# Graph kernel, gather passes: eight 32-column products of a tile become two of 128 columns

## The chip, the cores and the metric

The kernel runs on one core of a Trainium2 chip. The metric is the device time of one execution in microseconds; before the change the median of three runs is 7301.54 (7296.5 to 7303.85). The engines are TensorE (PE; its weight loads are listed as PEld), VectorE (DVE), ScalarE (ACT), GpSimd (POOL) and SyncE (SP).

## The reference, cut to what matters

3125 nodes with 256 features, 50000 edges (sorted by target), four graph layers one after the other, each with a residual and a layer normalisation. The first and the third sum over the edges of each target node, with a softmax weight:

```
# first layer (one head)
scores = h_src @ a_s + h_tgt @ a_t
ex = exp(scores - segment_max(scores, tgt)[tgt])
agg = segment_sum(h_src * (ex / (se[tgt] + 1e-10))[:, None], tgt)
# third layer (8 heads of 32 features, self loops added)
e = leaky_relu(a_src[src] + a_dst[dst], 0.2)
ex = exp(e - segment_max(e, dst)[dst])
out = segment_sum(h[src] * alpha[:, :, None], dst)
```

The second layer has three rounds of edge attention with 4 heads, the fourth multiplies by a product of 50000 plane rotations. None of the two is touched.

## The kernel before

The program sorts the edges by blocks of nodes, builds the rotation matrix, and then runs the layers in order. The function `segment_sums` holds one gather pass; it is called twice, with tag e0 and H=1 for the first layer and with tag e2 and H=8 for the third. A block is NBD = 32 target nodes. The edges stand in TD = 496 tiles of P = 128 edges, all of one block; four tiles are a batch, so there are NBT = 124 batches, and PER = 4 batches are a group. All main-loop code is written out, without a loop on the chip, and each engine has its own order, over steps `st` = 0 to 132:

- POOL (L1064 to L1074) fetches, with one indirect DMA for each tile, the 128 rows of the source nodes into `hg`, a ring of RING = 11 batches; from the twelfth batch on it first waits for "agg" of the batch 11 before.
- SP loads one-hot rows into `stack` (L1085).
- TensorE in step `st` first turns the score columns of batch `st` (L1152, into `ps_t`), then makes the logits of batch c = st-6 (L1161, into `ps_d`), then the control product of batch st-1 (L1170, into `ps_s`; one product for H=1, two of 128x512 for H=8), in one step of four a group's products (L1182, after a wait for VectorE's group work "A"), and last the gather of batch e = c-2 (L1193 to L1201) into one of two tiles `ps_g`. In one step of four the rescaling products L1209 and L1213 follow (for H=1 one, L1216).
- VectorE in step `st` takes a maximum from `ps_s` (L1244), adds the four results of batch c-3 from `ps_g` into `accT`, one after the other, at a block address read from a table (L1265), for H=8 makes the leaky logits (L1270, L1275), then the operand `Em` of batch c-1 (L1289), and after the last batch of a group the group work (L1297 to L1327, and the splitting into three bf16 parts in L1977 to L1981). Once in four steps it makes the one-hots `hot` of a group (L1282) and `spread` (L1334).
- ScalarE copies `ps_t` into `stack` (L1104), after L1182 copies `ps_x` to `R` (L1111), and takes the exponentials `exd` (L1132 or L1135).

`hot[p, tile, n]` is 1 where edge p of a tile belongs to node n of its block. In the gather, before the change, `Em` is this one-hot times the edge's exponential: 32 columns for H=1, 8 x 32 for H=8. For each 32 features the stationary operand is 32 columns of the gathered rows, and the moving one the 32 columns of `Em` (for H=8 those of that head). The four products of a half of the features write to partitions 0, 32, 64 and 96 of `ps_g`. L1199 makes the denominators. A float32 product appears in the trace as two records.

Of the kernel before, what the change touches and what calls it, by code (L numbers as in the profile page):

```python
# [12 lines left out]
P = 128  # L13
N, D, E = 3125, 256, 50000
# [13 lines left out]
NBD = 32  # L28
# [3 lines left out]
RING, ROWS, LAG = 11, 8, 6  # L32
# [889 lines left out]
def segment_sums(nc, tag, K, H, W, htab, adtab, estab, blocks, quads, ohtab, oth, kl, accT, selftab):  # L922
# [14 lines left out]
    PER = GT // 4  # L937
    STEPS = NBT + LAG + 3
    with ExitStack() as ctx:
# [95 lines left out]
        hg = sm("hg", [P, RING, 4, W])  # L1035
# [20 lines left out]
        with ExitStack() as rs:  # L1056
# [3 lines left out]
            with phase(nc, tag + "m", names, rings) as (block, s):  # L1060
# [76 lines left out]
                @block.tensor  # L1137
                def _(pe):
                    pe.wait_ge(s["zero"], 1)
                    for i in range(2):  # L1140
                        pe.matmul(ps_g[i][:, 0:2].rearrange("p u v n -> p (u v n)"), K["zero"][:, 0:P], K["zero"][:, 0:192],
                                  start=True, stop=True, skip_group_check=True)
                        pe.matmul(ps_g[i][:, 2:4].rearrange("p u v n -> p (u v n)"), K["zero"][:, 0:P], K["zero"][:, 0:192],
                                  start=True, stop=True, skip_group_check=True)
                    for st in range(STEPS):
                        c, b = st - LAG, st - 1
                        if st < NBT:
                            pe.wait_ge(rings[st % RING], 64 * (st // RING + 1))
                            if st >= 1:
                                pe.wait_ge(s["row"], st)  # L1150
                            for u in range(4):
                                tr = pe.matmul(ps_t[ROW0:ROW0 + SPLITS * H, u, :], hg[:, st % RING, u, D:W].bitcast(BF16)[:, 0:SPLITS * H],  # L1152
                                               K["identb"][:, :], start=True, stop=True)
                            tr.then_inc(s["turn"], 1)
                        if 0 <= c < NBT:
                            if c % PER == 0:
                                pe.wait_ge(s["R"], c // PER + 1)
                            if c >= 1:
                                pe.wait_ge(s["exd" if S2 == 1 else "dc"], c)
                            for u in range(4):  # L1160
                                mm = pe.matmul(ps_d[:, u, :], stack[:, c % ROWS, u, :],  # L1161
                                               R[:, c // PER % 2, (c % PER) * 4 + u, :], start=True, stop=True)
                            mm.then_inc(s["D"], 1)
                        if 0 <= b < NBT:
                            pe.wait_ge(s["row"], b + 1)
                            pe.wait_ge(oh_s[b % ROWS], 64 * (b // ROWS + 1))
                            if b >= 1:
                                pe.wait_ge(s["peak"], b)
                            for k in range(HC):
                                mm = pe.matmul(ps_s[0:M, k].rearrange("p u e -> p (u e)"), ctl[:, k, 0:M],  # L1170
                                               stack[:, b % ROWS].rearrange("p u e -> p (u e)"), start=True, stop=True)
                            mm.then_inc(s["ctl"], 1)
                        if st % PER == 1 and st >= PER + 1 and st // PER - 1 < NG:
                            g = st // PER - 1
                            pe.wait_ge(s["A"], g + 1)
                            if g >= 1:
                                pe.wait_ge(s["R"], g)
                            if S2 > 1:
                                pe.wait_ge(s["adst"], g + 1)
                            for h in range(H4):  # L1180
                                for n in range(SPLITS):
                                    mm = pe.matmul(ps_x[n * NBD:(n + 1) * NBD, h].rearrange("p s c t -> p (s c t)"),  # L1182
                                                   K["identb"][0:M, h * NBD:(h + 1) * NBD],
                                                   B[0:M, g % 2, n].rearrange("p s c t -> p (s c t)"), start=True, stop=True,
                                                   skip_group_check=True)
                            mm.then_inc(s["sel"], 1)
                        if 0 <= c - 2 < NBT:
                            e = c - 2
                            pe.wait_ge(s["E"], e + 1)
                            if e >= 2:  # L1190
                                pe.wait_ge(s["take"], (e - 2) * 4 + 4)
                            for u in range(4):
                                lhs = lambda lo, n: hg[:, e % RING, u, lo:lo + n]  # L1193
                                for k in range(2):
                                    for h in range(4):
                                        pe.matmul(ps_g[e % 2][h * NBD:(h + 1) * NBD, u, k, :], lhs(k * P + h * NBD, NBD),  # L1196
                                                  Em[:, e % 2, u, k * 4 + h if H > 1 else 0, :],
                                                  start=True, stop=True, skip_group_check=True)
                                mm = pe.matmul(ps_g[e % 2][0:H, u, 2, :], exd[:, e % 3, u, :],  # L1199
                                               hot[:, e // PER % 2, (e % PER) * 4 + u, :], start=True, stop=True,  # L1200
                                               skip_group_check=True)  # L1201
                            mm.then_inc(s["agg"], 1)
                            if (e + 1) % PER == 0 and (e + 1) // PER < NG:
                                g = (e + 1) // PER
                                pe.wait_ge(s["spread"], g)
                                if g >= 2:
                                    pe.wait_ge(s["grow"], g - 1)
                                if H > 1:
                                    pe.matmul(ps_y[:, 0:2, :].rearrange("p v n -> p (v n)"), quad[:, :],  # L1209
                                              spread[:, g % 2].rearrange("p c n -> p (c n)"), start=True, stop=True,  # L1210
                                              skip_group_check=True)
                                    for k in range(HC):
                                        mm = pe.matmul(ps_y[:, 2, :], quadden[:, k, :], spread[:, g % 2, k, :],  # L1213
                                                       start=(k == 0), stop=(k == HC - 1), skip_group_check=True)
                                else:
                                    mm = pe.matmul(ps_y[:, 0, :], K["ones"][0:M, :], spread[0:M, g % 2, 0, :], start=True,  # L1216
                                                   stop=True)
                                mm.then_inc(s["scale"], 1)

                @block.vector  # L1220
                def _(dve):
# [17 lines left out]
                    for st in range(STEPS):  # L1239
# [37 lines left out]
                        if 0 <= c < NBT:  # L1277
                            if c % PER == 0:
                                g = c // PER
                                if g >= 2:  # L1280
                                    dve.wait_ge(s["agg"], (g - 2) * PER + PER)
                                dve.tensor_tensor(hot[:, g % 2], K["row"][:, 0:NBD].unsqueeze(1).broadcast_to([P, GT, NBD]),  # L1282
                                                  kl[:, g * GT:(g + 1) * GT].unsqueeze(2).broadcast_to([P, GT, NBD]),
                                                  ALU.is_equal).then_inc(s["hot"], 1)
                            dve.wait_ge(s["exd"], c + 1)
                            dve.wait_ge(s["hot"], h0 + c // PER + 1)
                            if c >= 2:
                                dve.wait_ge(s["agg"], c - 1)
                            dve.tensor_tensor(Em[:, c % 2],  # L1289
                                              hot[:, c // PER % 2, (c % PER) * 4:(c % PER) * 4 + 4].unsqueeze(2)  # L1290
                                              .broadcast_to([P, 4, H, NBD]),
                                              exd[:, c % 3].unsqueeze(3).broadcast_to([P, 4, H, NBD]),
                                              ALU.mult).then_inc(s["E"], 1)
                        if 0 <= b < NBT and b % PER == PER - 1:
# [1056 lines left out]
```

## Time and profile before

| | |
|---|---|
| median of three runs | 7301.54 us |
| span of the profiled execution | 9062.1 us |
| own time of the profiled execution | none listed beside the span |
| mean granted TensorE clock | 0.812 |
| PE matmul busy | 4683.8 us (52%), 60555 instructions |
| DVE busy | 5139.2 us (57%), 12108 instructions |
| POOL busy | 4305.5 us (48%), 3974 instructions |
| L1196 gather products, both passes | 15872 records, 569.9 us busy |
| L1069 indirect DMA, both passes | 992, 991.8 us busy |

The profiled execution was longer than the timed ones. A slice of the page's second part is 226.6 us. The main loop of the first gather pass lies from about 2833 to 3690 us, that of the third layer from about 7919 to 8815 us.

### The profile page before, as it was taken

How to read it: one execution, taken by the hardware profiler on the slowest of the kernel's cores; microseconds unless marked ns; L12 is line 12 of the kernel's file. 1: busy time of each engine (PE TensorE's matmuls, PEld its weight loads, DVE VectorE, ACT ScalarE, POOL GpSimd, SP SyncE). 2: the span in 40 equal slices, each digit the busy share in tenths (PEclk: the TensorE clock that was granted, in tenths of full speed). 3: DMA queues.
4: the chain of work that ended last, by engine and by line, in shares of the span. 5: the costliest groups of instructions: out<-in, count | busy, mean ns of one | idle time of the engine just before them, and what ended most of it. 6: DMA issues, size and time to landing. Idle time of an engine off the chain costs nothing. (4 is left out here: it accounts for less than half of the span.)

```text
span 9062.1 us, 179398 instructions
## 1 busy us (share of the span) xinstructions
PE 4683.8 (52%) x60555; PEld 3816.1 (42%) x60555; DVE 5139.2 (57%) x12108; ACT 1224.9 (14%) x2828; POOL 4305.5 (48%) x3974
## 2 busy tenths in 40 slices
PE   0000000488732555476766767766676777445552
PEld 0000000366621444356666556666566665323331
DVE  7996000377754444655665455555455555557767
ACT  0000000122201111111111011111011111122220
POOL 5887777200063555135655055554255552066640
PEclk9999999999955555689999889898889988755555
DMA  0000000000012333155552255551355540133320
GB/s 24 3 1 1 1 1 1 1 0 0 4 26 65 101 101 101 48 167 156 158 157 62 88 147 161 152 150 31 117 154 158 156 120 21 30 94 98 98 75 24
DMA packets 708570, 691.60 MB, mean 76 GB/s; under 512 B 234981, under 2 KB 589355, under 8 KB 708165
## 3 DMA queue, kind: packets, MB, share of 16 engines
q0 software_dynamic: 227328, 446.06, 18.1%
q1 hardware_dynamic: 480846, 240.51, 9.6%
q8 instruction: 218, 3.57, 0.2%
q14 instruction: 178, 1.46, 0.1%
HBM read 766.03 MB, written 77.58 MB: 93 GB/s over the span
## 5 line engine op out<-in xcount | busy, mean ns | idle before, releaser
L1669 POOL DMA_INDIRECT kvring<-kvtab,oth x1776 | 1834.4, 1033 | 1619.5 <-PE ea_psg L1731 923.2
L1069 POOL DMA_INDIRECT e_hg<-htab,oth_d x992 | 991.8, 1000 | 1130.9 <-issue 713.4
L1720 PE MATMUL ea_pss<-ea_qb,ea_kT 128*128 128x128 f32 x7104 | 1198.0, 306 | 0.0
L1720 PEld LDWEIGHTS ea_pss<-ea_qb,ea_kT 128*128 128x128 f32 x7104 | 1113.8, 224 | 32.3
L1790 DVE TENSOR_TENSOR acc<-ea_psg,acc 128x64 f32 x1776 | 399.0, 225 | 1161.3 <-remote 1049.8
L1731 PE MATMUL ea_psg<-ea_mix,kvring 128*64 128x64 f32 x14208 | 581.9, 240 | 887.6 <-DVE ea_mix L1832 877.2
L1731 PEld LDWEIGHTS ea_psg<-ea_mix,kvring 128*64 128x64 f32 x14208 | 522.1, 152 | 984.8 <-issue 691.2
L255 POOL DMA_INDIRECT sb_rec<-srawrec,splacei x392 | 430.9, 1099 | 960.5 <-PEq L56 815.9
L1196 PE MATMUL e_psg<-e_Em,e_hg 128*32 128x32 f32 x15872 | 569.9, 245 | 439.6 <-issue 399.4
L1764 ACT ACTIVATE ea_kT<-ea_pst 128x512 f32<-128x512 f32 x888 | 481.9, 595 | 2201.5 <-remote 1331.3
L1196 PEld LDWEIGHTS e_psg<-e_Em,e_hg 128*32 128x32 f32 x15872 | 439.2, 146 | 622.0 <-issue 524.2
L241 POOL DMA_INDIRECT steps<-or_rec,or_rplacei x392 | 568.3, 1450 | 136.0 <-issue 136.0
L1804 DVE TENSOR_REDUCE ea_sc<-ea_pss 128x64 f32<-128x1024 f32 x444 | 541.6, 1220 | 97.6 <-PE ea_pss L1720 61.8
L1717 PE MATMUL ea_pss<-mrow,ea_mk 128*128 128x256 bf16 x1776 | 547.6, 308 | 64.7 <-ACT ea_kT L1764 49.0
L1832 DVE TENSOR_TENSOR ea_mix<-ea_hot,ea_att 128x1024 f32<-128x1024 f32 (+1 forms) x444 | 544.1, 1225 | 0.1
L1708 PE MATMUL ea_pst<-ident,kvring 128*128 128x128 f32 x3552 | 464.8, 274 | 78.4 <-DMA kvring<-kvtab,oth 77.3
L1244 DVE TENSOR_REDUCE e_mt<-e_pss 32x4 f32<-32x512 f32 (+1 forms) x248 | 235.0, 948 | 465.7 <-PE e_pss L1170 371.6
L237 POOL DMA_INDIRECT sd_rec<-drawrec,dplacei x392 | 406.2, 1036 | 128.4 <-issue 126.4
L1708 PEld LDWEIGHTS ea_pst<-ident,kvring 128*128 128x128 f32 x3552 | 406.4, 142 | 80.5 <-issue 79.4
L1265 DVE TENSOR_TENSOR accT<-e_psg,accT 128x96 f32 x992 | 254.3, 256 | 253.5 <-issue 131.4
L594 DVE TENSOR_TENSOR or_T<-or_psw,or_T 128x512 f32<-128x512 f32 x97 | 66.8, 689 | 451.8 <-remote 424.7
L1199 PE MATMUL e_psg<-e_hot,e_exd 128*1 128x32 f32 (+1 forms) x1984 | 291.5, 239 | 34.9 <-issue 34.9
(506 smaller groups left out, 8250.9 us busy)
## 6 DMA issues: line engine op xcount, KB each, us to landing
ea_qb<-qtab SPq DMA_DIRECT2D x1776, 64.0 KB
qtab<-at_qst SPq DMA_DIRECT2D x75, 512.0 KB, 3.3
kvring<-kvtab,oth POOLq DMA_INDIRECT x1776
e_stack<-ohtab SPq DMA_DIRECT2D x744, 32.0 KB
kvtab<-at_kvst SPq DMA_DIRECT2D x75, 256.0 KB, 2.7
e_hg<-htab,oth_d POOLq DMA_INDIRECT x992
ea_mk<-mtab SPq DMA_DIRECT2D x444, 3.0 KB
htab<-Hd SPq DMA_DIRECT2D x2, 3200.0 KB, 11.6
```

What stands on the lines that cost most here:

```text
L241: pool.indirect_dma_start(out=rec, out_offset=bass.IndirectOffsetOnAxis(ap=placei[:, j:j + 1], axis=0), in_=rawrec[:, j, :], in_offset=Non ...
L255: pool.indirect_dma_start(out=rec, out_offset=bass.IndirectOffsetOnAxis(ap=placei[:, begin + j:begin + j + 1], axis=0), in_=rawrec[:, begi ...
L1069: pool.indirect_dma_start(out=hg[:, b % RING, u, :], out_offset=None, in_=htab, in_offset=bass.IndirectOffsetOnAxis(ap=oth[:, b * 4 + u:b ...
L1196: pe.matmul(ps_g[e % 2][h * NBD:(h + 1) * NBD, u, k, :], lhs(k * P + h * NBD, NBD), Em[:, e % 2, u, k * 4 + h if H > 1 else 0, :], start=T ...
L1669: pool.indirect_dma_start(out=kv[:, b % R, u, :], out_offset=None, in_=kvtab, in_offset=bass.IndirectOffsetOnAxis(ap=oth[:, b * QB + u:b * ...
L1708: tr = pe.transpose(ps_t[:, u, k, :], kv[:, r, u, k * P:(k + 1) * P], K["ident"][:, :])
L1717: pe.matmul(ps_s[r % 2][:, u, :], mk[:, r, u * P:(u + 1) * P], K["mrow"][:, :], start=True, stop=False, skip_group_check=True)
L1720: mm = pe.matmul(ps_s[r % 2][:, u, k * 2 * HN:(k + 1) * 2 * HN], kT[:, r % 2, u, k, :], qb[:, r, u, :], start=False, stop=True, skip_group ...
L1731: mm = pe.matmul(ps_g[r % 2][c * DH1:(c + 1) * DH1, u, :], kv[:, r, u, D + g * DH1:D + (g + 1) * DH1], mix[:, r % 2, u, g * G:(g + 1) * G, ...
L1764: ins = act.activation(kT[:, r % 2, 2 * k:2 * k + 2], ps_t[:, 2 * k:2 * k + 2], ACT.Copy)
L1804: dve.tensor_reduce(sc[:, :, :, :].rearrange("p u g h -> p (u g h)"), ps_s[r % 2][:, :, :].rearrange("p u (q n) -> p (u q) n", n=NBS), AX. ...
L1832: dve.tensor_tensor(mix[:, r % 2], hot[:, bass.ds(b * QB, QB), :].unsqueeze(2) .broadcast_to([P, QB, G * G, NBS]), att[:, :, :, :].rearran ...
```

## The change

In `segment_sums` the gather's products are regrouped. For H=1 the stationary operand is 128 features of the gathered rows at once and the moving one the 32 columns of `Em`. For H=8 VectorE multiplies the gathered rows themselves by the exponentials (each head's on its 32 features), so that `Em` is 256 weighted features; TensorE has 128 of these columns as stationary operand, and the one-hots of the tile, unweighted, as the moving one. The result in `ps_g` stands at the same place as before.

```diff
@@ -1190,14 +1190,16 @@
                             for u in range(4):
-                                lhs = lambda lo, n: hg[:, e % RING, u, lo:lo + n]
+                                nodes = hot[:, e // PER % 2, (e % PER) * 4 + u, :]
                                 for k in range(2):
-                                    for h in range(4):
-                                        pe.matmul(ps_g[e % 2][h * NBD:(h + 1) * NBD, u, k, :], lhs(k * P + h * NBD, NBD),
-                                                  Em[:, e % 2, u, k * 4 + h if H > 1 else 0, :],
+                                    if H > 1:
+                                        pe.matmul(ps_g[e % 2][:, u, k, :], Em[:, e % 2, u, k * 4:(k + 1) * 4, :]
+                                                  .rearrange("p h n -> p (h n)"), nodes,
                                                   start=True, stop=True, skip_group_check=True)
-                                mm = pe.matmul(ps_g[e % 2][0:H, u, 2, :], exd[:, e % 3, u, :],
-                                               hot[:, e // PER % 2, (e % PER) * 4 + u, :], start=True, stop=True,
+                                    else:
+                                        pe.matmul(ps_g[e % 2][:, u, k, :], hg[:, e % RING, u, k * P:(k + 1) * P],
+                                                  Em[:, e % 2, u, 0, :], start=True, stop=True, skip_group_check=True)
+                                mm = pe.matmul(ps_g[e % 2][0:H, u, 2, :], exd[:, e % 3, u, :], nodes, start=True, stop=True,
                                                skip_group_check=True)
@@ -1287,8 +1289,8 @@
                             dve.tensor_tensor(Em[:, c % 2],
-                                              hot[:, c // PER % 2, (c % PER) * 4:(c % PER) * 4 + 4].unsqueeze(2)
-                                              .broadcast_to([P, 4, H, NBD]),
+                                              hg[:, c % RING, :, 0:D].rearrange("p u (h d) -> p u h d", h=H) if H > 1 else
+                                              hot[:, c // PER % 2, (c % PER) * 4:(c % PER) * 4 + 4].unsqueeze(2),
                                               exd[:, c % 3].unsqueeze(3).broadcast_to([P, 4, H, NBD]),
                                               ALU.mult).then_inc(s["E"], 1)
```

## Rows read from the trace of the kernel before

**Rows 1.** The page: the span, and two rows of the 40 slices.
```profile
span 9062.1 us, 179398 instructions
...
POOL 5887777200063555135655055554255552066640
PEclk9999999999955555689999889898889988755555
```

**Rows 2.** Windows of rotations, first pass, third layer, its tail; busy, granted clock.
```profile
core 0: us, PE busy (x) PEld busy (x) DVE busy (x) ACT busy (x) POOL busy (x), PEclk, DMA share, GB/s
3200.00:3300.00 100.00, 58.88 (x1268) 41.62 (x1267) 43.32 (x152) 13.10 (x39) 58.30 (x61) 0.50 0.38 101
...
8350.00:8450.00 100.00, 57.27 (x1295) 36.75 (x1293) 73.80 (x190) 25.44 (x61) 61.48 (x59) 0.50 0.36 97
8842.00:8856.00 14.00, 8.98 (x33) 5.01 (x33) 9.41 (x13) 1.28 (x1) 0.00 (x0) 0.50 0.07 4
1900.00:2000.00 100.00, 84.70 (x1123) 68.95 (x1123) 76.47 (x185) 22.62 (x48) 0.00 (x0) 0.95 0.01 0
```

**Rows 3.** Timeline of the first pass: start, length, engine, line, operation, count, idle before.
```profile
3204.03 0.30 PE L1196 MATMUL e_psg<-e_Em,e_hg 128*32 128x32 f32 x3 [0.39 <-issue]
...
3204.52 0.95 POOL L1069 DMA_INDIRECT e_hg<-htab,oth_d  x1 [0.30 <-issue]
...
3206.25 0.24 PE L1196 MATMUL e_psg<-e_Em,e_hg 128*32 128x32 f32 x1 [0.50 <-issue]
...
3207.69 0.46 PE L1196 MATMUL e_psg<-e_Em,e_hg 128*32 128x32 f32 x16
```

**Rows 4.** Groups by form, 2900 to 3860 us: busy, mean ns, idle before, releasers.
```profile
L1069 POOL DMA_INDIRECT e_hg<-htab,oth_d x452 | 436.7, 966 | 313.0 <-PE e_psg L1199 209.7 <-issue 102.9 <-DMA e_hg<-htab,oth_d 0.3
L1196 PE MATMUL e_psg<-e_Em,e_hg 128*32 128x32 f32 x7936 | 328.9, 245 | 279.6 <-issue 268.7 <-DVE e_Em L1289 10.6
```

**Rows 5.** Timeline of TensorE in the third layer's pass.
```profile
8128.74 1.01 PE L1213 MATMUL e_psy<-e_spread,e_quadden 128*128 128x32 f32 x4
8129.68 0.60 PE L1152 MATMUL e_pst<-identb,e_hg 128*24 128x128 bf16 x4
8130.22 0.28 PE L1161 MATMUL e_psd<-e_R,e_stack 128*128 128x16 bf16 x4
8130.34 1.01 PE L1170 MATMUL e_pss<-e_stack,e_ctl 128*128 128x512 bf16 x2
8131.29 0.44 PE L1196 MATMUL e_psg<-e_Em,e_hg 128*32 128x32 f32 x16
8131.52 0.24 PE L1199 MATMUL e_psg<-e_hot,e_exd 128*8 128x32 f32 x1
...
8131.84 0.24 PE L1199 MATMUL e_psg<-e_hot,e_exd 128*8 128x32 f32 x1
...
8131.90 0.24 PE L1199 MATMUL e_psg<-e_hot,e_exd 128*8 128x32 f32 x1
```

**Rows 6.** Timeline of VectorE in the third layer's pass, over two and a half steps.
```profile
8294.13 1.22 DVE L1244 TENSOR_REDUCE e_mt<-e_pss 128x8 f32<-128x1024 f32 x1 [2.83 <-PE e_pss L1170]
...
8303.39 1.22 DVE L1244 TENSOR_REDUCE e_mt<-e_pss 128x8 f32<-128x1024 f32 x1
...
8307.49 1.22 DVE L1289 TENSOR_TENSOR e_Em<-e_hot,e_exd 128x1024 f32<-128x1024 f32 x1
8308.64 1.22 DVE L1244 TENSOR_REDUCE e_mt<-e_pss 128x8 f32<-128x1024 f32 x1
...
8310.86 0.26 DVE L1265 TENSOR_TENSOR accT<-e_psg,accT 128x96 f32 x1 [0.29 <-DVE accT L1265]
...
8313.27 1.21 DVE L1244 TENSOR_REDUCE e_mt<-e_pss 128x8 f32<-128x1024 f32 x1
```

**Rows 7.** The same stretch, the group's products and what follows them.
```profile
8303.08 0.40 PE L1182 MATMUL e_psx<-e_B,identb 128*32 128x64 bf16 x12 [3.89 <-DVEq L1323]
...
8303.98 2.50 ACT L1111 ACTIVATE e_R<-e_psx 64x256 bf16<-64x256 f32 x2 [5.24 <-PE e_psx L1182]
...
8307.27 0.25 PE L1161 MATMUL e_psd<-e_R,e_stack 128*128 128x16 bf16 x4 [2.15 <-ACT e_dsb L1126]
```

## The prediction

> **What bounds the kernel now.** I read the slices first, then windows, the groups by form, and timelines. The slices show two stretches of interest with TensorE's clock at 0.5 throughout: slices 13 to 16 and 36 to 39 [rows 1]. These are the main loops of the first gather pass (H=1, tag e0) and of the third layer's (H=8, tag e2), 124 batches of four tiles each. Only they hold lines 1193 to 1200 and 1289, so only they change. In the windows POOL starts 61 gathers in 100 us of the first pass and 59 in the third layer's [rows 2]; a batch has four, so a batch lasts 6.56 and 6.8 us there. A pass has 82 matmul records a batch outside the group work, and 1268 in 100 us are 6.5 us a batch, the value I use for both.
>
> Two things must be separated. The profiled span is 9062.1 us; no separate time of that execution is listed, so the span is its time here; the median of the runs that count is 7301.5, or 1760.6 us less. The recorded execution therefore holds waits that the timed ones do not. The timeline of the first pass shows where such waits may sit: after a dense stretch TensorE takes one to three L1196 matmuls every 0.7 us with "issue" before them, so waits for nothing, and then sixteen in 0.46 us [rows 3]. I read this as the recording holding the engine back: the gaps follow the number of matmuls, not a semaphore. L1196 has 7936 matmuls in a pass (each of the 8 products of a tile is two records) and 268.7 us of "issue" before them in the first pass [rows 4].
>
> Without those gaps the first pass is bound by POOL: one gather is 0.95 us with 0.30 before it [rows 3], four are 5.0 us. TensorE needs about 2.6 us for a batch (below), VectorE about 3.7: 43.32 us busy per 15.25 batches [rows 2] is 2.84, and three gaps of 0.29 between its four dependent additions [rows 6] bring 0.9 more.
>
> The third layer's pass is bound by VectorE. Reductions of L1244 start at 8294.13, 8303.39, 8308.64 and 8313.27 [rows 6]: the step that ends a group of four batches takes 9.26 us, the next two 5.25 and 4.63, and only one of them has a wait for TensorE before it (2.83 us, in front of 8294.13, again behind a trickle). With a fourth step of about 5.1 (4.4 plus the one-hots of a group, 0.7) a group is 24.2 us, 6.05 a batch.
>
> **What the change does to TensorE.** Per tile, eight products become two; as records, 16 become 4, and per pass 7936 become 1984. The instruction count falls by three quarters. The work does not. The old products had 32 stationary columns and wrote to four different 32-partition strips. Their pitch: L1199 of one tile starts at 8131.52, of the next at 8131.84 [rows 5], so a tile with its 16 records and two denominators takes 0.32 us and a batch 1.3. Four strips run beside each other; one record costs under 0.02 us.
>
> The new products have 128 stationary columns in f32 and 32 moving ones. This is exactly the form of L1213 (128x128 stationary, 32 moving, f32), in the same pass and at the same 0.50 clock: four records from 8128.74 to 8129.68, 0.235 us each [rows 5]. A batch has 16 such records: 3.76 us. Its eight L1199 records stay, 0.055 each (8131.84 to 8131.90), 0.44. So the gather of a batch goes from 1.3 to 4.2 us of TensorE time. It matters little whether the stationary operand is the gathered row (first pass) or the weighted row (third layer): both are 128 wide.
>
> The Trainium skill's page TensorEngine Tiling, section Performance Considerations, speaks against this edit: a stationary side of 32 columns is the case for four column tiles, with up to four times the speed. The rows agree and show more than the factor of four, 0.32 against 0.94 for a tile's gathers with the same sums. The page TensorE: Matmul & The Clock Gate of the Trainium skill, section LDWEIGHTS, gives columns divided by 1.2 ns for a load, 107 ns for 128; by it 16 records would be an estimated 1.7 us, a batch 3.3 to 3.8, and the edit would cost nothing. L1213 takes 0.235 in f32, and I go by that.
>
> **First pass, sum.** Besides the gather TensorE has, per batch, L1152 0.54 us (8129.68 to 8130.22), L1161 0.12 to 0.2, L1170 half of the 0.95 seen in the third layer (8130.34 to 8131.29, two products; here one) [rows 5], and a share of the group's products, 0.15. Before: 1.3 + 1.3 = 2.6. After: 4.2 + 1.3 = 5.5, above POOL's 5.0. TensorE becomes the bound, and POOL waits for its "agg" to free a ring slot: +0.5 x 124 = +62 us. Bounds: if all of POOL's 0.30 is also recording, the timed pass runs at POOL's busy time, 3.8 (VectorE's 3.7 just below), and the cost is +1.7 x 124 = +211; if the 6.5 us a batch of the recording were real, 6.5 to 5.5 is -124. I take +75, near POOL's row. VectorE's 128-element L1289 only loses a broadcast of length one: nothing.
>
> **Third layer, sum.** VectorE's L1289 stays one 1024-element f32 product; only its first operand is now hg instead of a broadcast one-hot. I cost it at nothing; were it 0.1 us slower it would be +12 us if VectorE bound. Between slower and faster by 0.1 is its range. It needs no new wait: exd already comes from the row that hg brought. TensorE's step is 4.2 + 0.54 + 0.12 + 0.95 = 5.8 us. Over a group: 4 x 5.8 = 23.2, plus L1209 and L1213 1.4, plus the small L1182 0.4 [rows 7], 25.0. To this comes an idle stretch that cannot be filled: L1182 waits for VectorE's group chain, which ends 8.95 us after the L1244 of that step starts (8294.13 to 8303.08) [rows 6, 7], while TensorE has 5.8 us of work from the same moment: 3.2 us idle. The following wait, L1161 for ACT's L1111 (8303.08 to 8307.27) [rows 7], is now under the longer gather (4.2). Sum 28.2, or 7.05 a batch against 6.05: +1.0 x 124 = +124 us, rounded to +130 for semaphore steps. Bounds: +0.55 x 124 = +68 if the recording's 6.5 was real, and +200 if VectorE without recording ran a group in 22 us.
>
> Both: +75 + 130 = +205, 7301.5 + 205 = **7506**. In the recorded execution, whose trickle the shorter stream should end, the same paces give about -124 and +68, so its span should fall by some 56 us, to about 9006, while the timed runs get slower. The span is no guide for this change.
>
> **Rivals.**
> *The clock rises.* After the change TensorE is busy without a break in the first pass, and where it is so elsewhere it has the higher level: 0.95 in the rotations, 84.70 us busy of 100 [rows 2]. At 2.4 GHz a batch's TensorE time is 2.8 and 3.3 us: POOL and VectorE bind as before, 7301 (-15 to +20). Against it: in the tail of the third layer, where TensorE transposes with f32 loads of 128 columns, 8.98 us busy of 14, the level is 0.50, and in neither pass does it leave 0.5 [rows 1, 2]; in the new stream nearly all the time is loading, with only 32 columns streamed behind it. Chance 0.08. The rule behind this rival is in the Trainium skill, page TensorE: Matmul & The Clock Gate, Part 1: sustained activity releases the slow clock. The trace agrees for the rotations only.
>
> *Issue really is the limit (the other side).* If the gaps of [rows 3] are the engine's own and happen in every run, three quarters of L1196 gone takes them out. With the slow clock: -124 + 68 = -56, 7246. With the fast one: first pass 6.5 to 5.0, -186, third layer 6.5 to 6.05, -56, 7060. It decides when an unrecorded batch of the first pass takes over 5.5 us. For it: the gaps are in the trace and POOL waits 209.7 us for L1199 [rows 4]. Against: 1760 us must be missing somewhere, and a burst of 16 in 0.46 us right behind the gaps shows that the instructions were at hand. Chance 0.10, a third of it the fast clock.
>
> *Loads are cheaper than L1213's row* (hidden behind the previous product), so TensorE stays under POOL: 7301 to 7340. Its four in a row should have shown it. Chance 0.04.
>
> **How the numbers follow.** My forecast, TensorE-bound at the lower clock in both passes, has 0.78. Its own range: the lows +62 and +68 give 7431, the highs +211 and +200 would give 7713, of which I cut the top, as both together are unlikely: 7410 to 7620. With the cases at no change taken in, 7295 to 7620. A measurement tells about 0.2% (15 us) from nothing. Faster 0.11, same 0.08, slower 0.81.
>
> **What would show it.** The new gather products: 1984 records a pass with a pitch near 0.235 at clock 0.50; TensorE at 9 tenths in slices 13 to 16; 18 gathers of POOL per 25 us in the first pass (5.5 a batch) and 14 in the third layer (7.05); VectorE with waits for L1170 in front of L1244 at every step; L1289 at 1.22 us. Wrong it would be if the granted clock in these passes reads near 1.0, if the new records pitch at 0.13 or less, or if the timed median falls below 7290.

## The result and the profile after

The changed kernel takes 7601.1 us (four runs, 7599.87 to 7602.31) against 7299.24: ratio 1.0406 [1.0393, 1.0419], 302 us slower. The forecast was slower, 7506, range 7295 to 7620. All times here and below are of the faster of two states that executions show; one of the four runs of `after_interleaved` (7689.51, mean granted clock 0.688 against 0.812) was in the slower one and is left out of its time.

The rows that answer to [rows 1]; a slice is now 190 us:

```profile
span 7598.9 us, 155590 instructions
...
PE   0000488864399995788886888867887872888971
...
PEclk9999999985555557999998999989999986555555
```

Counted from 1, as the prediction counts them, TensorE stands at 9 tenths in the slices of the first pass (12 to 15) and at 8 to 9 in the third layer's (35 to 38), the granted clock at 0.50 (1.2 GHz) as before. The span agrees with the timed runs. The 9062.1 us of the kernel before was that one recording's: the same kernel recorded again (`before_again`) had a span of 7307.0, as its timed runs have. So its windows are the ones to hold against the changed kernel's. Columns as in [rows 2], first `before_again`, then the changed kernel; the first window of each is in the first pass, the second in the third layer:

```profile
2200.00:2300.00 100.00, 56.69 (x1645) 41.76 (x1645) 58.16 (x203) 18.02 (x55) 75.93 (x80) 0.50 0.49 131
6700.00:6800.00 100.00, 56.31 (x1472) 36.22 (x1472) 81.34 (x209) 28.90 (x72) 73.67 (x67) 0.50 0.42 111
```

```profile
2200.00:2300.00 100.00, 98.58 (x559) 77.09 (x560) 47.04 (x168) 14.40 (x44) 63.08 (x66) 0.50 0.40 107
...
6700.00:6800.00 100.00, 88.16 (x528) 69.83 (x528) 69.53 (x182) 23.54 (x55) 52.25 (x54) 0.50 0.34 91
```

PE is up from 57 to 99 and from 56 to 88 us of 100, with a third of the records; POOL's gathers fall from 80 to 66 and from 67 to 54. Where each pass starts and ends is in the groups of the gather's products by form (records, min/median/max ns, first and last start). `before_again`, both passes, then the changed kernel:

```profile
L1196 PE MATMUL e_psg<-e_Em,e_hg x7936: 209/241/263, 2064.9 to 2674.9; 128*32 128x32 f32 x199
L1196 PE MATMUL e_psg<-e_Em,e_hg x7936: 196/241/264, 6330.9 to 7056.3; 128*32 128x32 f32 x199
```

```profile
L1200 PE MATMUL e_psg<-e_Em,e_hg x1984: 401/401/423, 2063.0 to 2815.8; 128*128 128x32 f32 x199
...
L1196 PE MATMUL e_psg<-e_hot,e_Em x1984: 261/401/423, 6469.9 to 7350.0; 128*128 128x32 f32 x199
```

The first pass goes from 610.0 to 752.8 us (+142.8), the third layer from 725.4 to 880.1 (+154.7). Together 297.5 of the 302. By the count of 124 batches: 4.92 to 6.07 and 5.85 to 7.10 us a batch. These lengths, last start less first, are used for every kernel below.

TensorE in the changed kernel's first pass, one batch and the start of the next (start, length, operation, count). L1200 are the new products, L1202 the denominators:

```profile
2296.25 1.06 PE L1200 MATMUL e_psg<-e_Em,e_hg 128*128 128x32 f32 x4
2297.25 0.26 PE L1202 MATMUL e_psg<-e_hot,e_exd 128*1 128x32 f32 x2
2297.44 1.06 PE L1200 MATMUL e_psg<-e_Em,e_hg 128*128 128x32 f32 x4
...
2299.81 1.06 PE L1200 MATMUL e_psg<-e_Em,e_hg 128*128 128x32 f32 x4
2300.81 0.21 PE L1202 MATMUL e_psg<-e_hot,e_exd 128*1 128x32 f32 x1
2300.81 0.26 PE L1152 MATMUL e_pst<-identb,e_hg 128*3 128x128 bf16 x1
...
2301.33 0.27 PE L1161 MATMUL e_psd<-e_R,e_stack 128*128 128x1 bf16 x4
2301.52 0.61 PE L1170 MATMUL e_pss<-e_stack,e_ctl 128*32 128x512 bf16 x1
2302.06 1.06 PE L1200 MATMUL e_psg<-e_Em,e_hg 128*128 128x32 f32 x4
```

No row has idle time before it. Read the starts, not the lengths, which overlap: four records of a tile take 1.00 us (2296.25 to 2297.25), its two denominators 0.19, a tile 1.19. The gather is 4.56 (to L1152 at 2300.81; the last tile's denominators lie beside L1152), the whole batch 5.81.

The third layer at the end of a group (the changed kernel, TensorE, VectorE and ScalarE; L1246 is the old L1244):

```profile
6699.71 1.22 DVE L1246 TENSOR_REDUCE e_mt<-e_pss 128x8 f32<-128x1024 f32 x1 [2.24 <-PE e_pss L1170]
6708.54 0.40 PE L1182 MATMUL e_psx<-e_B,identb 128*32 128x64 bf16 x12 [2.96 <-DVEq L1325]
6708.87 1.06 PE L1196 MATMUL e_psg<-e_hot,e_Em 128*128 128x32 f32 x4
...
6714.01 0.28 PE L1161 MATMUL e_psd<-e_R,e_stack 128*128 128x16 bf16 x4
6715.19 1.23 DVE L1246 TENSOR_REDUCE e_mt<-e_pss 128x8 f32<-128x1024 f32 x1 [1.33 <-PE e_pss L1170]
...
6719.91 0.27 PE L1161 MATMUL e_psd<-e_R,e_stack 128*128 128x16 bf16 x4
...
6721.09 1.23 DVE L1246 TENSOR_REDUCE e_mt<-e_pss 128x8 f32<-128x1024 f32 x1 [1.26 <-PE e_pss L1170]
...
6728.62 1.23 DVE L1246 TENSOR_REDUCE e_mt<-e_pss 128x8 f32<-128x1024 f32 x1 [2.24 <-PE e_pss L1170]
```

A group is 28.91 us (6699.71 to 6728.62), a plain step 5.90 (L1161 to L1161), and VectorE waits for L1170 in front of the reductions shown. In the step with the group's work TensorE stands still 2.96 us before L1182, then L1161 follows without a wait for ScalarE [rows 7 had 2.15].

### The profile page after: what moved, and what is told of

It reads as the page before. It is cut to its first block and busy times, and to the rows that moved or that the text cites. A ratio compares the mean times of both kernels' runs of the same rounds, so it can differ in the third digit from the quotient of the medians.

```text
span 7598.9 us, 155590 instructions
## 1 busy us (share of the span) xinstructions
PE 5125.4 (67%) x48651; PEld 4185.9 (55%) x48651; DVE 5147.1 (68%) x12108; ACT 1178.9 (16%) x2828; POOL 4435.4 (58%) x3974
## 5 line engine op out<-in xcount | busy, mean ns | idle before, releaser
L1671 POOL DMA_INDIRECT kvring<-kvtab,oth x1776 | 1998.4, 1125 | 818.9 <-issue 427.5
L1722 PE MATMUL ea_pss<-ea_qb,ea_kT 128*128 128x128 f32 x7104 | 1024.5, 277 | 0.0
L1722 PEld LDWEIGHTS ea_pss<-ea_qb,ea_kT 128*128 128x128 f32 x7104 | 950.4, 194 | 16.7
L1246 DVE TENSOR_REDUCE e_mt<-e_pss 32x4 f32<-32x512 f32 (+1 forms) x248 | 235.7, 950 | 450.5 <-PE e_pss L1170 450.3
L1733 PE MATMUL ea_psg<-ea_mix,kvring 128*64 128x64 f32 x14208 | 523.9, 228 | 13.7 <-DVE ea_mix L1834 13.3
L1719 PE MATMUL ea_pss<-mrow,ea_mk 128*128 128x256 bf16 x1776 | 493.0, 278 | 55.8 <-ACT ea_kT L1766 22.2
L1200 PE MATMUL e_psg<-e_Em,e_hg 128*128 128x32 f32 x1984 | 527.0, 406 | 0.0
L1196 PEld LDWEIGHTS e_psg<-e_hot,e_Em 128*128 128x128 f32 x1984 | 476.0, 325 | 73.7 <-issue 24.0
L1196 PE MATMUL e_psg<-e_hot,e_Em 128*128 128x32 f32 x1984 | 513.3, 399 | 0.0
L1733 PEld LDWEIGHTS ea_psg<-ea_mix,kvring 128*64 128x64 f32 x14208 | 462.0, 140 | 89.1 <-issue 86.3
L1200 PEld LDWEIGHTS e_psg<-e_Em,e_hg 128*128 128x128 f32 x1984 | 460.3, 322 | 79.9 <-issue 38.5
L1267 DVE TENSOR_TENSOR accT<-e_psg,accT 128x96 f32 x992 | 255.0, 257 | 277.0 <-DVE accT L1267 226.2
```

Source lines behind the costliest of these rows:

```text
L1196: pe.matmul(ps_g[e % 2][:, u, k, :], Em[:, e % 2, u, k * 4:(k + 1) * 4, :] .rearrange("p h n -> p (h n)"), nodes, start=True, stop=True, s ...
L1200: pe.matmul(ps_g[e % 2][:, u, k, :], hg[:, e % RING, u, k * P:(k + 1) * P], Em[:, e % 2, u, 0, :], start=True, stop=True, skip_group_check ...
L1671: pool.indirect_dma_start(out=kv[:, b % R, u, :], out_offset=None, in_=kvtab, in_offset=bass.IndirectOffsetOnAxis(ap=oth[:, b * QB + u:b * ...
L1719: pe.matmul(ps_s[r % 2][:, u, :], mk[:, r, u * P:(u + 1) * P], K["mrow"][:, :], start=True, stop=False, skip_group_check=True)
L1722: mm = pe.matmul(ps_s[r % 2][:, u, k * 2 * HN:(k + 1) * 2 * HN], kT[:, r % 2, u, k, :], qb[:, r, u, :], start=False, stop=True, skip_group ...
L1733: mm = pe.matmul(ps_g[r % 2][c * DH1:(c + 1) * DH1, u, :], kv[:, r, u, D + g * DH1:D + (g + 1) * DH1], mix[:, r % 2, u, g * G:(g + 1) * G, ...
```

## The experiments

Below, "first" and "third" are pass lengths; before is 610.0 and 725.4, the changed kernel 752.8 and 880.1. Batch costs divide by 124.

**The two halves of the change.** `first_only` gives the 128-column products to H=1 only, `third_only` to H>1 only, `strips_weighted_rows` keeps VectorE's edit for H=8 and computes it with eight 32-column products (in both passes; cut to the two operands):

```diff
+ lhs = Em[:, e % 2, u, k * 4 + h, :] if H > 1 else hg[:, e % RING, u, k * P + h * NBD:k * P + (h + 1) * NBD]
+ rhs = nodes if H > 1 else Em[:, e % 2, u, 0, :]
```

> Only the first pass (H=1) has the two 128-column products. Theory (TensorE's weight loads at the lower clock set the pace): the trace of after shows 66 gathers in 100 us, 6.1 us a batch; POOL alone would allow 5.0, so +1.1 x 124 = +135 us, 7435. Rival (the cost sits in the third layer, in VectorE's reading of gathered rows or its chain): within 20 us of before.

> Only the third layer (H=8) is changed, VectorE's edit and the 128-column products. Theory: the rest of the 302 us, +165, 7465, with a batch at 7.2 us. Rival (the two passes disturb each other's stages, or one carries all): not additive with first_only.

> Third layer only: VectorE weights gathered rows as in after, but TensorE keeps eight products of 32 stationary columns, into four strips; the first pass as before. Theory: VectorE's edit costs nothing, 7300 +-15. Rival (VectorE's edit is what costs: another operand, or hg held longer): +100 us or more.

> The kernel before, unchanged, profiled once more. If its span of 9062 was that one recording's (waits that the timed runs do not have), the span is now near 7300 or differs by hundreds; the first pass then runs at 5.0 us a batch (80 gathers in 100 us) and the third layer near 5.9. Rival (the issue gaps belong to the engine): span 9062 again and 6.5 us a batch in both passes.

Measured: `first_only` 7443.19, ratio 1.0192 [1.0173, 1.0211], +140; `third_only` 7454.99, 1.021 [1.0191, 1.0229], +152; `strips_weighted_rows` 7309.61, 1.0009 [0.9998, 1.0019]; `before_again` 7307.16, 1.0004 [0.9993, 1.0015]. The two passes add (292 of 302). VectorE's edit costs nothing that can be told from noise; the loss is the form of TensorE's products.

**Is instruction count or TensorE's work the limit?** `before_doubled` issues every old product twice; the second overwrites the first, so the sums are unchanged (the expectation's "doubled" was a slip). `after_half` leaves one of the two new products of a tile out.

```diff
-for k in range(2):
+for k in (0, 0, 1, 1):      # before_doubled, from the kernel before
+for k in range(1):          # after_half, from the changed kernel
```

> Each of the eight 32-column products of a tile is issued twice (16 instead of 8), so TensorE's gather of a batch of four tiles does twice the products and twice the instructions. The sums come out doubled; the time is what is read. Theory (TensorE has slack, what bounds is GpSimd's gathers in the first pass and VectorE in the third layer): the gather goes from 1.3 to about 2.6 us a batch, TensorE's batch from 2.6 to 3.9 us against 5.0 in the first pass, so nothing there (80 gathers in 100 us as before); in the third layer TensorE's batch is at most some 5 us against VectorE's 5.9, where part of the gather stands in the chain from the products to VectorE's additions: 0 to +50 us, 7300 to 7350. Rival (what counts is the issue of TensorE's many short instructions): 16 more products a tile-pair with their records at the issue pitch of before, +1.3 us a batch in both passes, 2 x 124 x 1.3 = +320 us, about 7625.

> The changed kernel with one of the two 128-column products of each tile left out, so half of the features are not summed. Theory (TensorE's gather with its 128-column float32 loads is what bounds both passes): the gather of a batch goes from 4 x (4 x 0.247 + 0.20) = 4.75 us to 4 x (2 x 0.247 + 0.20) = 2.8 us; TensorE's first pass batch from 6.1 to 4.1 us, under GpSimd's 5.0, so 80 gathers in 100 us again; in the third layer TensorE's 7.2 goes to 5.2, under VectorE's 5.9: 7300, at most 7330. Rival (the loss is not in the products but in the longer chain rows, products, additions, or in the form of the weighted rows): the time stays near 7500 to 7600.

Measured: `before_doubled` 7328.3, ratio 1.0036 [1.0024, 1.0048], first 621.5, third 736.5. In its first pass a tile with 32 records takes 0.52 us (denominators at 2303.82 and 2304.35). 15872 records more cost 23 us, so issue is no limit. The clock is not the same, though: the tile just read ran at 0.50, but the first pass of `before_doubled` as a whole has a mean granted clock of 0.69 (2070 to 2670 us), where the kernel before has 0.50. Part of the added work was so done at the higher level. At 0.50 throughout it would be 4 x (0.52 - 0.32) = 0.8 us a batch, 3.4 instead of the prediction's 2.6 and still under POOL's 4.92 (an estimate from these rows). `after_half` 7335.2, ratio 1.0041 [1.0026, 1.0057], first 613.7, third 755.8: halving the new work brings the first pass back whole, the third layer to +30. The whole kernel is 5 us over the expectation's bound. What the +30 is stays open.

**Order of the denominators.** `after_den_last` is the changed kernel with a batch's four denominators behind its eight products.

```diff
+                            for u in range(4):
+                                nodes = hot[:, e // PER % 2, (e % PER) * 4 + u, :]
                                 mm = pe.matmul(ps_g[e % 2][0:H, u, 2, :], exd[:, e % 3, u, :], nodes, ...
```

> The changed kernel with the four denominators of a batch issued after its eight products, not one behind each tile's two products. Theory (the 0.20 us that each tile's denominator costs, 1.19 less 4 records of 0.247, is mostly the turn from a 128-column load to a one-column one and back, which three of four tiles are spared): 0.09 us less for each of three tiles, 0.3 us a batch, 2 x 124 x 0.3 = -70 us, 7530; between 7500 and 7580. Rival (a denominator costs its 0.20 wherever it stands): 7600. A second rival (the products of one tile run into those of the next without a gap once nothing stands between, the loads hidden): more than -120, 7480 or less.

Measured: 7448.05, ratio 1.0197 [1.0181, 1.0213], first 681.4, third 809.8: 153 us less than the changed kernel, twice the expectation. Its TensorE, a plain batch of the first pass and one that ends a group:

```profile
2299.59 3.62 PE L1200 MATMUL e_psg<-e_Em,e_hg 128*128 128x32 f32 x16
2303.14 0.42 PE L1204 MATMUL e_psg<-e_hot,e_exd 128*1 128x32 f32 x5
2303.33 0.27 PE L1152 MATMUL e_pst<-identb,e_hg 128*3 128x128 bf16 x1
...
2304.58 3.62 PE L1200 MATMUL e_psg<-e_Em,e_hg 128*128 128x32 f32 x16
2308.13 0.58 PE L1204 MATMUL e_psg<-e_hot,e_exd 128*1 128x32 f32 x8
2308.65 0.63 PE L1220 MATMUL e_psy<-e_spread,ones 32*128 32x32 f32 x2
```

Sixteen records in a row take 3.55 us, 0.222 each, and eight denominators 0.52. So a 128-column record is still not hidden (the second rival's number came, its reason did not); a turn between the two shapes costs on both sides. A plain batch takes 4.99 us (2299.59 to 2304.58) instead of 5.81, that is 0.82 less. The passes fell by 0.58 and 0.57 us a batch. In the first pass most of the rest went back into the wait for VectorE at L1182, which is longer now:

```profile
PE e_psx L1182 <- DVEq L1325: 13.5, 29, 1.2
```

```profile
PE e_psx L1182 <- DVEq L1327: 37.8, 29, 1.9
```

The first line is the changed kernel, the second `after_den_last`: 24.3 us more, 0.20 a batch.

**Why were the old products cheap: width or strips?** `strip_by_strip` is the kernel before with the 32 products ordered strip after strip; `two_strips_64` the changed kernel with four 64-column products.

```diff
+for h in range(4):           # strip_by_strip: strip outermost
+    for u in range(4):
+        for k in range(2):
+for h in range(2):           # two_strips_64, inside for k
+    out = ps_g[e % 2][h * 64:(h + 1) * 64, u, k, :]
```

> The kernel before with the same 32 products of a batch in another order: first all eight of strip 0 (four tiles, two halves), then those of strip 1, 2 and 3, then the four denominators. Count, width and results are unchanged; only neighbours in the stream now share a strip. Theory (the old products are cheap because four strips work side by side: 16 records in 0.32 us are 4 of 0.08 in each strip): 64 records one after another, 64 x 0.08 = 5.1 us a batch and 0.5 for the denominators against 1.3, so TensorE's batch is some 6.9 us in the first pass (bound there 5.0) and some 8 in the third layer (5.9): about +240 and +260, 7800. Rival (the old products are cheap because a 32-column record costs a quarter of a 128-column one, 0.222 / 4 = 0.055 us, wherever it goes): 64 x 0.055 + 0.5 = 4.0 us, first pass 5.3 against 5.0, third layer 6.5 against 5.9: +35 and +75, 7410. Second rival (order is nothing, records issue at 0.02 us each as now): 7300.

> The changed kernel with four 64-column products of a tile in two strips of 64 in place of two of 128 columns; everything else as in the changed kernel. Theory (cost of a record grows with its columns, and strips work side by side): four records of 0.11 to 0.12 us in each of two strips, 0.45 to 0.5 us a tile, and 0.2 for the denominator: 2.7 us a batch, TensorE's batch 4.0 in the first pass (bound 5.0 by GpSimd), about 5.2 in the third layer (5.9 by VectorE): 7300 to 7340. Rival (a record's cost is the same 0.22 to 0.25 us at 64 columns as at 128, and two strips side by side): 4 x 0.235 + 0.2 = 1.15 us a tile, as the changed kernel: 7600. Second rival (records of 64 columns at 0.12 us but one after another): 8 x 0.12 + 0.2 = 1.15 us, again 7600.

Measured: `strip_by_strip` 7302.54, ratio 1.0003 [0.9993, 1.0012], first 609.6, third 727.3; `two_strips_64` 7336.9, ratio 1.0054 [1.0037, 1.007], first 613.5, third 760.5. Two gathers of `strip_by_strip`, then the windows of the two (their granted clock is the third number from the end, 1.00 and 0.50), then one tile of `two_strips_64`, at 0.50:

```profile
2299.92 1.79 PE L1195 MATMUL e_psg<-e_Em,e_hg 128*32 128x32 f32 x61
2301.53 0.19 PE L1200 MATMUL e_psg<-e_hot,e_exd 128*1 128x32 f32 x1
...
2311.31 2.90 PE L1195 MATMUL e_psg<-e_Em,e_hg 128*32 128x32 f32 x61
2313.98 0.27 PE L1200 MATMUL e_psg<-e_hot,e_exd 128*1 128x32 f32 x2
```

```profile
2299.92:2301.53 1.61, 1.61 (x63) 1.60 (x62) 0.94 (x2) 0.46 (x2) 1.21 (x2) 1.00 0.48 126
...
2311.31:2313.98 2.67, 2.67 (x64) 2.67 (x62) 1.58 (x7) 0.73 (x4) 2.06 (x3) 0.50 0.52 135
```

```profile
2303.38 0.64 PE L1202 MATMUL e_psg<-e_Em,e_hg 128*64 128x32 f32 x8
2303.95 0.26 PE L1204 MATMUL e_psg<-e_hot,e_exd 128*1 128x32 f32 x2
```

61 records one after another in one strip at a time take 1.61 us at clock 1.00 and 2.67 at 0.50, 0.026 and 0.044 each; with neighbours in different strips a record takes 0.020 at 0.50 [rows 5]. I had expected 0.08 for a strip alone. It is half of that, so strips side by side bring a factor of about 2.2 and not 4. The 500 us that the theory priced did not come either: at 0.50 a whole batch of this order takes 4.08 us (2311.31 to 2315.39, where the next gather starts), under POOL's 4.92.

A 64-column record is 0.57/8 = 0.071. Per tile, all at 0.50 and with the same 512 columns loaded in all, products alone: at most 0.32 us at 32 columns with strips side by side (the old tile, its denominators included), 0.70 at 32 columns in one strip (16 x 0.044), 0.57 at 64 in two strips, 0.89 to 1.00 at 128 (4 x 0.222 to 0.25). So the change lost in two ways. What strips side by side save, 0.38 us a tile or a little more, is gone, and this is the larger part. The wider record costs the other 0.19 to 0.30: one of 128 columns takes 0.222 to 0.25, four of 32 in one strip 0.175. How much of the 64-column price is its width and how much its two strips was not separated, nor what the third layer's +35 in `two_strips_64` is.

**What bounds the third layer?** `before_interleaved` and `after_interleaved` put VectorE's four additions (L1265, L1267) between the maximum, the logits and `Em`, so that none waits 0.29 for the one before it.

```diff
+take(0)
 maximum        # L1244
+take(1)
 lx             # L1270
+take(2)
 dx, hot, Em    # L1275, L1282, L1289
+take(3)
```

> The kernel before, with VectorE's four additions into accT of a batch no longer back to back but each put between the operations of the softmax (maximum, lx, dx, Em), so that each one's wait for the one before it is over. TensorE's work is that of before. Theory (VectorE bounds the third layer, its batch of 5.9 us is its own operations and three waits of 0.29 us between the additions): up to 3 x 0.29 = 0.87 us a batch less, 124 x 0.87 = -108 at most; -50 to -108, 7195 to 7250; the first pass stays at 80 gathers in 100 us. Rival (the third layer of the kernel before is set by the turn from rows over TensorE's products to VectorE and back, not by how long VectorE's operations take): no change or slower, 7300 to 7350.

> The changed kernel with the same interleaving of VectorE's four additions that brought the kernel before to 7242 us. Theory (in the changed kernel TensorE's gather bounds both passes and VectorE waits in every step of the third layer, 2.2, 1.3 and 1.3 us in one group for L1170): shorter VectorE work has nothing to give in the first pass and little in the third layer, only where VectorE's chain of a group's third batch holds L1182 (2.96 us once a group; 0.37 to 0.9 us of it back, 31 groups): -12 to -28, 7570 to 7590. Rival (the third layer of the changed kernel is bound by the round trip products, additions, next products, in which VectorE counts in full): 124 x 0.4 to 0.8 = -50 to -100, 7500 to 7550.

Measured: `before_interleaved` 7242.07, ratio 0.9917 [0.9904, 0.9931], first 607.9, third 677.6: VectorE does bound the old third layer (-48 us, 0.39 a batch; not the full 0.87). Of the 63 us gained 13 lie outside the two lengths. It is faster than both kernels. `after_interleaved` 7539.12, the median of three, ratio 1.033 [1.0311, 1.0352], 62 less than the changed kernel, 51 of them in the two lengths; first 737.7, third 844.3. I had said 12 to 28; the rival's 50 to 100 came. The waits of TensorE on VectorE's chain, third layer, changed kernel and then `after_interleaved` (us, times, longest):

```profile
PE e_psx L1182 <- DVEq L1325: 82.9, 28, 3.0
```

```profile
PE e_psx L1182 <- DVEq L1337: 48.8, 28, 2.8
```

2.96 us a group became 1.74. That is 1.22 x 31 = 38 us, and the third layer gained 36. The same wait in the first pass was 13.5 us over 29 groups and is 0.2 now, nearly all of the 15 us gained there. So the place was right, once a group at L1182, and the size was wrong: 1.22 is more than the 0.87 of one step's three waits. My reading is that the chain holds the waits of more than one step; that is not shown. The rival's round trip in every step is not seen; TensorE has no wait there.

## Why the prediction was right, and where its sizes were off

- **POOL bounds the first pass of before, 5.0 us a batch** from 0.95 + 0.30: right, 80 gathers in 100 us, 4.92 by length. The bound of 3.8 (all of the 0.30 being recording) falls.
- **VectorE bounds the third layer, 6.05**: right in kind (`before_interleaved`), 5.85 measured. That 0.20 is 25 us of the miss.
- **The recording holds the engine back**: right in that the gaps belong to one recording, `before_again` has 7307.0 and 16 of the old records every 0.32 us without the trickle. What held the first recording back is not known. The step built on it failed: that the next recording would also be held, with a span near 9006. It was 7598.9. Two recordings of one kernel differed by 1755 us, and I had taken one recording's waits for a property of every recording.
- **The new record priced by L1213, 0.235 us**: right within 6%; 0.25 between denominators, 0.222 in a row. This step carries the forecast's sign. The Trainium skill, page TensorE: Matmul & The Clock Gate, section LDWEIGHTS, gives the columns divided by 1.2 as a load's ns. By it 16 records of 128 columns would be an estimated 1.7 us. The trace does not agree for these float32 records, which took 3.55 to 4.0.
- **The gather after, 3.76 + 0.44 = 4.2**: measured 4.56. The 16 records took 4.00 (0.25 each between denominators), which is 0.24 of the miss. A pair of denominators between them costs 0.19, not 0.11; three of the four pairs count, 0.57, which is the other 0.13.
- **The first pass after, 5.5**: measured 6.07, +143 instead of +75, the largest miss. Of the 0.57, 0.36 is the gather; 0.11 a wait for VectorE at L1182 (13.5 us over 29 groups) that my sum did not have; the rest are small excesses of L1170 (0.54) and of the group's products.
- **The third layer after, 7.05**: measured 7.10. A step was forecast at 5.8 and is 5.90, the idle stretch before L1182 3.2 and is 2.96, and the wait for L1111 went under the gather as said. Mostly the base was off, hence +155 instead of +130. That the step came so near is in part luck: its gather took 4.44 (6714.94 to 6719.38) and not 4.2, but L1161 and L1170 together 0.93 and not 1.07.
- **VectorE's weighting of gathered rows at nothing**: right, L1291 takes 1.22 us, `strips_weighted_rows` is within 0.2%.
- **Rivals.** Clock rises: no, 0.50 throughout with PE 99 us busy of 100. Issue is the limit: excluded by `before_doubled`. Loads cheaper: no. The Trainium skill, page TensorEngine Tiling, section Performance Considerations, spoke for four column tiles at 32 columns, and the traces agree in the direction: 0.32 us a tile with strips side by side, 0.70 without (`strip_by_strip`), 0.89 to 1.00 at 128 columns. The prediction's words that the rows show more than the factor of four are wrong: 0.94 against 0.32 is a factor of 2.9. Nothing was added up from that, nor from its 3.3 us a batch of the third layer at the higher clock, which by its own 25.0 us a group would be 3.1.

The sum: 75 + 130 forecast, 143 + 155 measured; of the 93 missing, 68 are the first pass and 25 the third layer. The cause and the order of events were right. The size was two thirds of what came, inside a range that was wide.

## What to carry to other kernels

Price a product by a row of its own shape: here, with a float32 stationary side and 32 moving columns, the cost followed the stationary columns and whether neighbours lay in different strips, and fewer, wider products held the engine longer than many narrow ones. Compare such prices only at the same granted clock: one price of this case is 0.026 or 0.044 by the clock alone. A count of instructions is no cost until doubling it moves the time. Before arguing from a span that does not match the timed runs, record the kernel again.

## What the runs showed of the hardware that was not expected

- A 32-column float32 record costs 0.026 us (granted clock 1.00) or 0.044 (0.50) alone in its strip. At 0.50 it costs 0.020 with neighbours in other strips, 0.016 in `before_doubled` (32 in 0.52 us, denominators included). A 64-column one in two strips costs 0.071, a 128-column one 0.222 to 0.25, both at 0.50.
- Alternating 128-column with one-column float32 products made a plain batch of the first pass 5.81 us against 4.99 with the shapes kept apart, and cost 153 us over the kernel.
- `strip_by_strip` ran its first pass at a mean granted clock of 0.80, with 70 us busy of 100, `before_doubled` at 0.69 with 66, the kernel before at 0.50 with 57, and the changed kernel at 0.50 with 99: busy time in the trace does not tell which level (1.2 or 2.4 GHz) is granted. The two means between the levels are stretches at either.
